# Moving value products, the denominator's product and q's projection in the PE program of an attention stage

## The reference

```python
qkv = x_ln @ w_qkv.T                                    # x_ln: 16 images, 1024 tokens, 64 channels
q, k, v = (to_heads(t) for t in jnp.split(qkv, 3, -1))  # 8 heads of 32 channels
scores = jnp.einsum('bhqd,bhkd->bhqk', q, k) * 32 ** -0.5
attn = jax.nn.softmax(scores, axis=-1)
out = jnp.einsum('bhqk,bhkd->bhqd', attn, v)
```

## Time and profile before

| | |
|---|---|
| runs | 3499.21, 3495.88, 3499.93 us |
| profiled execution, its span | 3492.03 us, 3490.3 us |
| PE, DVE, ACT, POOL busy over the span | 88%, 72%, 59%, 62% |
| exponentials of the attention | 101.9 us to 1792.2 us of the span |

### The profile page before, as it was taken

How to read it: one execution, slowest core, us unless ns; L and a number is a source line. 1 busy time by engine, 2 the same in 40 slices (tenths; PEclk the granted TensorE clock), 3 DMA queues, 4 the chain that set the end, 5 groups by cost and what they waited for, 6 DMA issues and landing times. The chain is left out here.

```text
span 3490.3 us, 54609 instructions
## 1 busy us (share of the span) xinstructions
PE 3056.1 (88%) x17526; PEld 1156.3 (33%) x17526; DVE 2526.1 (72%) x3282; ACT 2045.6 (59%) x2445; POOL 2163.6 (62%) x876
## 2 busy tenths in 40 slices
PE   5999999999999999999957999556887788877877
PEld 2333333333333333333312333422232222222222
DVE  4888888888788888888812221236898889898888
ACT  3577777777677777777732332235556545655554
POOL 0588888888778888888870000016666766676665
PEclk7899999999999999999979999778999999999999
DMA  3577777777767777777763210134343434434343
GB/s 108 121 170 173 185 170 178 184 172 172 172 168 177 176 179 172 176 185 173 170 149 111 94 42 12 63 116 152 124 154 126 146 129 143 146 127 163 109 158 121
DMA packets 111603, 503.25 MB, mean 144 GB/s; under 512 B 17184, under 2 KB 18276, under 8 KB 78516
## 3 DMA queue, kind: packets, MB, share of 16 engines
q0 software_dynamic: 32704, 218.17, 29.9%
q1 hardware_dynamic: 78676, 282.17, 23.5%
HBM read 192.42 MB, written 39.39 MB: 66 GB/s over the span
## 5 line engine op out<-in xcount | busy, mean ns | idle before, releaser
L565 DVE TENSOR_REDUCE at_pmax<-at_ring 128x1 f32<-128x512 f32 x2048 | 1289.2, 685 | 280.2 <-PE at_ring L356 279.0
L527 ACT ACTIVATE at_probs<-at_sc 128x1024 f32<-128x1024 f32 x1024 | 992.5, 1021 | 371.1 <-PE at_sc L423 369.6
L615 POOL TENSOR_TENSOR at_prob_sums<-at_prob_sums,at_probs 128x2048 f32<-128x2048 f32 x192 | 907.1, 4725 | 72.2 <-ACT at_probs L527 71.9
L416 PE MATMUL at_sc<-at_QT,at_KT 32*128 32x512 f32 x4096 | 774.4, 632 | 8.3 <-issue 7.1
L1695 POOL TENSOR_TENSOR ss_drive<-ss_du,ss_bsb 128x1024 f32<-128x1024 f32 x261 | 610.7, 2353 | 263.4 <-DVE ss_state L1652 256.6
L1595 ACT ACTIVATE ss_decay<-ss_delta,ss_a 128x512 f32<-128x512 f32 x520 | 354.5, 687 | 446.9 <-DVE ss_state L1648 298.9
L435 PE MATMUL at_O<-at_probs,at_V 128*32 128x512 f32 x4096 | 536.2, 607 | 1.1 <-ACT at_probs L527 1.1
L1484 PE MATMUL ss_Y<-ss_seen,ss_ident 128*128 128x512 f32 x1032 | 520.1, 628 | 0.0
L356 PE MATMUL at_ring<-at_KH,at_QH 32*128 32x512 bf16 x2048 | 430.1, 387 | 6.9 <-DVE at_pmax L565 4.0
L1660 DVE TENSOR_TENSOR ss_seen<-ss_state,ss_C 128x1024 f32<-128x1024 f32 x259 | 316.3, 1221 | 78.7 <-PE ss_C L1472 70.8
L1652 DVE TENSOR_TENSOR_SCAN ss_state<-ss_decay,ss_state,ss_drive 128x512 f32<-128x512 f32 x259 | 332.3, 1283 | 33.6
(11 more groups left out here) (195 smaller groups left out, 2847.7 us busy)
## 6 DMA issues: line engine op xcount, KB each, us to landing
ss_bsb<-scratch_rows SPq DMA_DIRECT2D x265, 512.0 KB, 6.9
at_odd_sums<-at_probs POOLq DMA_DIRECT2D x128, 1024.0 KB, 7.6
at_odd_sums<-at_probs SPq DMA_DIRECT2D x64, 1024.0 KB, 4.8
at_prob_sums<-at_odd_sums POOLq DMA_DIRECT2D x64, 1024.0 KB, 8.1
scratch_attn<-at_att SPq DMA_DIRECT2D x64, 256.0 KB, 2.0
fc_att<-scratch_attn SPq DMA_DIRECT2D x32, 512.0 KB, 5.8
ss_xn<-scratch_xm SPq DMA_DIRECT2D x34, 256.0 KB, 5.6
at_xn<-scratch_xn SPq DMA_DIRECT2D x32, 256.0 KB, 6.5
```

Of the source, the lines that this page charges most:

```text
L416: nc.tensor.matmul(sc[:, h, :], KT[head(h), par, blk(kb)], QT[head(h), par, hs(half)], start=True, stop=False)
L527: nc.scalar.activation(probs[:, kb, two, :].rearrange("p h q -> p (h q)"), sc[:, two, :].rearrange("p h q -> p (h q)"), ACT.Exp, scale=SCA ...
L565: nc.vector.tensor_reduce(pmax[:, quad // 2, h, quad % 2:quad % 2 + 1], ring[:, unit[3], :], AX_X, ALU.max, negate=True).then_inc(max_done, 1)
L615: nc.gpsimd.tensor_tensor(prob_sums[:, half, :, :], before, probs[:, POOL_ADDS[n], :, :], ALU.add).then_inc(pool_sums, 1)
```

## The change

It moves instructions in PE's program and adds or removes none. Of the key blocks' value products, blocks 0 and 1 stood together in step 2 of each half, blocks 2 and 3 alone in steps 3 and 4; now block 0 stands in step 2, block 1 in step 3, and blocks 2 and 3 together in step 4. The denominator's product (steps 6 and 14) stands ahead of the step's value product and no longer behind it. In step 0, the value product (of block 7 of the half before) stands ahead of q's projection. The programs of ACT, DVE, POOL and SP stay as they are.

```diff
-    PV_AT = {0: (LAST_KB,), 2: (0, 1), 3: (2,), 4: (3,), 5: (4,), 6: (5,), 7: (6,)}
+    PV_AT = {0: (LAST_KB,), 2: (0,), 3: (1,), 4: (2, 3), 5: (4,), 6: (5,), 7: (6,)}
@@
                     for kind, which in extra.get(s, []):
-                        if kind in MADE_AHEAD:
+                        if kind in MADE_AHEAD and kb:
                             project(stage, grp, par, kind, which)
+                        if kind == "den" and stage != "lead":
+                            denominators(stage, grp, which)
                     if stage != "lead":
                         for k in PV_AT.get(kb, ()):
                             if kb:
@@
                     for kind, which in extra.get(s, []):
                         if kind == "turn":
                             turn(stage, grp, which)
-                        if kind == "den" and stage != "lead":
-                            denominators(stage, grp, which)
+                        if kind in MADE_AHEAD and not kb:
+                            project(stage, grp, par, kind, which)
                     maxima(stage, grp, par, s, (2, 3))
```

## The result

The changed kernel took 3502.28 us (median of 20 runs, 3496.67 to 3511.5), the kernel before, in 20 runs beside it, 3495.84 us (3491.48 to 3505.88). The ratio is 1.0017 with a 95% interval of 1.001 to 1.0025: 6.4 us slower. The interval leaves out 1, so the loss is real, but it is smaller than the 0.2% under which the prediction speaks of no difference. The profiled execution took 3498.75 us with a span of 3497.1 us.

A forecast was written before the change was run, and what follows sets the result against it. PE's program was taken to set a group's length (busy 52.13 of 52.35 us). Value products 0, denominator 0 and q's projection 5.4 us, added to the runs' median 3499.2, gave 3504.6 us; range 3492 to 3519.

The forecast's parts named there:

- The likeliest case: Whole kernel: 0 + 0 + 5.4 us, so 3504.6 us, own range 3500 to 3509; chance 0.60.
- q's projection: Step 0, groups 1 to 30: later copy of q delays step 1's first maximum 0.19 us, taken as 0.18, 5.4 us.
- The other bounds: Step 0 exchange: 0.05 a group (1.5 us) with 0.86 before the projection; 0.3 (9 us) if DVE's reductions decide.
- The value products: Steps 2 to 4 of each half: moving them is worth 0, within 0.02 us a half.
- One sign: Trace after: forecast wrong if steps 5 and 6, or 11 and 12, don't sum to what they did.
- Step 5: First half: 0.66 us shorter because no longer late, with step 6 longer by that.
- The denominator: Steps 6 and 14: product 0.86 earlier costs 0; in step 14, 0.7 us stay after its sum's DMA lands.
- rival of the late steps: Two: one late step disappears, 3485 us, chance 0.12; late steps 3 and 11 aren't made up, 3522, chance 0.13.
- late step: Step whose value product waits for last step's exponentials' end + 1.33, not scores + 1.49; late by up to 0.67 us.
- the first rival: First half, steps 5 and 6: up to 0.66 x 30 = 20 us come back, 3485 us; chance 0.12.
- the lead: First half: PE runs 0.85 us earlier in steps 3 and 4, until step 4's two value products spend it.
- The order of starts on PE: By strict program order on PE, late steps cost about 0.1 us more, some 3 us, 3507.6; given no chance.

The follow-up runs named there:

- the held casts: Kernel before, without ACT's wait for the cast and with DVE casting one step later from the SBUF copy: 57.8 us a group, ratio 1.0458.

## Why the prediction was right

The forecast was 3504.6 us, 5.4 above before; measured are 3502.28 and 6.4 above before. The likeliest case, a small loss from q's exchange and nothing else, under 0.2%, is what happened.

- **Where the absolute number comes from.** The base was 3.4 us too high: the three runs of before had a median of 3499.21, and 20 runs had 3495.84. The difference was forecast 1.0 us too small. That the two errors partly cancel, down to 2.3 us, is luck.
- **q's projection: right, in each link.** Forecast 0.19 a group, taken as 0.18; measured 0.21 in step 1 and in no other, alone and in the whole. The links, on the times of group 11 less 1.75: projection 1.00 behind the value product (forecast 1.00), cast 684.61 (forecast 684.61), copy 685.34 (685.33), maximum 685.99 (685.97). The other bounds fell: like shapes did not make it 0.86, and DVE's reductions did not decide. That it is the wait on the cast is shown by the cast moved to step 4: -0.37 a group at the same order on PE.
- **The value products: right, 0.** Alone they measure 52.37 against 52.36. Step 3's projection stands at 694.40 (692.65 on the clock of before, forecast 692.44 without q's 0.21), step 4 keeps two products from 697.95, step 6's large product comes at 704.46, which is 701.19 + 1.94 + 1.33 with the exponential of step 5 in the row below. In the second half the products of steps 11 and 12 start at

```profile
720.31 1.06 PE L435 MATMUL at_O<-at_probs,at_V 128*32 128x512 f32 x8
...
723.18 1.92 PE L435 MATMUL at_O<-at_probs,at_V 128*32 128x512 f32 x16
```

  which, less 1.75 and q's 0.21, is 718.35 and 721.22, as forecast.
- **One sign was put down wrongly.** By the prediction it would be wrong if steps 11 and 12 didn't sum to what they did. They don't: 6.52 instead of 5.66. But its own working says so, since step 10 is 0.86 shorter and that comes back in steps 11 and 12; the sum to look at was that of steps 10 to 12, 9.40 both before and after.
- **Step 5: off by 0.18, with no effect.** Forecast 0.66 shorter, measured 0.48. The scores of step 6 start at 702.49, 1.19 behind the value product at 701.30, not 1.00. The last maximum of step 5 waits for its bank, since DVE makes the combination of the maxima (L575) ahead of the reduction that frees it:

```profile
701.55 0.23 DVE L575 TENSOR_REDUCE at_negm<-at_pmax 128x16 bf16<-128x32 f32 x1
```
```profile
701.19 1.94 ACT L529 ACTIVATE at_probs<-at_sc 128x1024 f32<-128x1024 f32 x2 [1.42 <-PE at_sc L423]
```

  Step 6 is bound by those exponentials, so it swallows the 0.18. Had step 6 not been late, this would have been a cost missed.
- **The denominator: 0 was right for the whole, and not for the reason given.** The prediction named one cover, the landing of the DMA, and followed nothing else in front of that product; it left out that the product takes a bank of the ring. Alone the move costs 0.35 us a group by exactly this wait, and only the table of the value products takes it away. In step 6 of the kernel after 0.33 us lie between the last reduction and the product, 0.2 more than the 0.14 that such a start needs. So the 0 for this edit was luck as far as the ring goes. The cover that the prediction did name held. Waits of PE's weight loads in the kernel after, 113 to 1717 us (in that stretch of before there is none):

```profile
PEld at_ring L408 <- DMA at_prob_sums<-at_odd_sums: 2.6, 4, 0.6
```

  These 4 stand in step 14, and there the sum landed 0.61 us or more ahead of the product; the step is 3.83 in these groups as in their neighbours. So they cost nothing, and the smallest cover is about the 0.7 us that the prediction worked out.
- **The rivals.** Neither rival of the late steps came true: steps 2 to 7 and steps 8 to 15 sum as before. The gain of the first rival exists, but with another table (two products in step 3): there the lead is spent in the late step itself.
- **The order of starts on PE.** The rule of the Trainium skill ("TensorE: Matmul & The Clock Gate", section "Part 3: Packing small matmuls") that matmuls start strictly in program order had no chance beside the forecast. The prediction puts 0.1 us a late step on it without a working. By it the values alone would have made a group 52.47 us; it is 52.37, against 52.36.

## What to carry to other kernels

Where engines run in lockstep, write down the few start-to-start rules of a step, say which of two waits ends last, and follow them until the lead is spent: for q's exchange and the tables of value products that came within 0.03 us a group, a gain included. It fails where a wait is left out of the list: the ring's bank cost 0.35 us a group, the held casts 5.4. When a step is moved, go through all that it waits for, the bank it takes as well as the data, since the neighbour that went first may have been hiding a wait that only now shows. Two edits that each pay or cost alone may act on the same wait, so measure the pair before adding them up.

## What the runs showed of the hardware

- A cast on DVE from float32 in SBUF to bfloat16 (128x512) takes 0.42 us alone, but when it starts amid POOL's addition of 4.81 us it ends only 0.3 us behind that: 3.75 and 3.77 us in the rows, 5.09 at most. The cast from PSUM takes 0.68 to 0.69 us and isn't held in any of 114 that start amid an addition; nor are ACT's copies from SBUF, 0.63 us, 65 of which do. The shorter instruction was the more expensive one, by 5.4 us a group.
- Between shapes that follow each other on PE the spacing differs: 1.00 from a value product to other work, but 0.88 from the denominator's product to the value product (704.46 to 705.34; 706.02 to 706.89 is 0.87), which has its shape.
- The start of matmuls needn't follow the program: in the earlier trace rows two maxima start at 699.02, ahead of second passes of the scores at 699.25 that stand before them. No run here shows what that is worth.
